# Adding an output bias on POOL ahead of time, and writing a marker one step earlier

## The chip, the cores and the metric

The kernel is one program on one core of a Trainium2 chip. Time is device microseconds of one execution, from a median of several runs; lower is better. Engines are named as in the profile: PE (TensorE), DVE (VectorE), ACT (ScalarE), POOL (GpSimd) and SP (SyncE, which here only issues DMAs). Each engine runs its own instructions strictly in the order written, and they are tied together by semaphores: an instruction adds one to a semaphore when it is done (`then_inc`), another engine waits until it has reached a value (`wait_ge`).

## What is computed

Two layers, each an attention with few keys followed by a mixture of experts (MoE), over 2048 tokens of 128 channels. Only the first attention matters here; of it, for `x` of shape (2048, 128):

```python
q = (layernorm(x) @ Wq + bq)            # 16 heads of 8 channels, each head's q scaled to length 1
attn = softmax(q @ k.T * scale + attn_bias)   # 77 keys for each of 4 batches
x = x + (attn @ v) @ Wo + bo            # bo: one row of 128 numbers, the same for all tokens
```

Behind it `layernorm(x)` goes to a router that picks 2 of 8 experts for each token.

## The kernel before

The tokens are 16 tiles of 128 (`NT`), one partition per token; `x` stays in SBUF for the whole kernel. Both attention stages are software pipelines, written as one function for each engine and step, `step0(i)` for the first stage, called for i = 0 to 23. In step i an engine works on several tiles at once: each block in the function has a line `t = i - k`, which says how many steps behind tile t stands there. The order of the blocks in the function is the order on that engine's queue, and it was laid out by hand. So each engine's step is a fixed list, and a wait in one block holds up all blocks behind it.

The blocks around the change, for tile t:

- DVE makes xnA (L918, the first LayerNorm's result) in step t + 1, from `x`. Until x's add nothing else reads `x` of that tile but this and the statistics before it.
- PE makes q, the scores S (L1378, L1381), transposes the probabilities (L1408, L1419, L1435), multiplies them with the values (L1467), and then, in step t + 7, multiplies the result with Wo into PSUM (L1428). A second product follows into the same place (L1429): a row of ones times the row `bo`, which adds the bias to all 128 tokens. Both are f32 and go as two passes each.
- DVE adds this to `x` (L902, step t + 7), takes mean and variance (L924 to L945), and makes `pays`, the normalised rows that will be sent to the experts, twice (L1018). `pays` needs rsD, the variance to the power -0.5, from POOL.
- PE transposes `pays` (L1388, step t + 8), ACT copies it to x2T (L673), PE makes the router's scores (L1459), DVE picks the two experts and counts ranks until the slot numbers of each token stand in `slots` (L1004, step t + 8).
- `pays` also has one more column, the marker, which says where the row comes from. ACT writes it from `dest` (L676, step t + 8, right behind x2T). Before that ACT waits until the scatters of tile t - 4 are done, since four buffers of `pays` go round.
- POOL scatters the rows into DRAM by the slot numbers with two indirect DMAs (L495), after waits for the marker and the slot numbers.

POOL's step in this order: rsD of tile i - 6 (L482), in steps 0 to 3 the power for four tiles of the first LayerNorm (L485), the two scatters of tile i - 7, and qr, the power -0.5 for the lengths of q, of tile i - 1 (L502). POOL's steps lie beside later ones of DVE: POOL's step i waits for what DVE makes in step i + 1 and at the start of step i + 2.

DVE's step, from L902 on: x's add, the scores minus their maximum (L908, L910), xnA, statistics and routing in turn, 1/denominator (L981, waits for PE's L1467), the attention output `on` (L998), slot numbers (L1004), `qn` (L1009, q times qr), `pays` (L1018), qsm (L876), `big` (L882), the maxima (L890, L891), q plus its bias (L896), and x's add again.

After step 23 DVE works out which expert each of 39 blocks of 128 rows belongs to, SP waits for the last scatters, and the first MoE reads the rows back. `bo_bc` holds `bo` broadcast to all 128 partitions; the kernel before uses only its first partition.

Of the kernel before, what the change touches and what calls it, by code (L numbers as in the profile page):

```python
# [34 lines left out]
ALU = mybir.AluOpType  # L35
# [9 lines left out]
def bass_xattn_moe_two_layers(nc, x_in, ctx_in, bias_in, Wq0, bq0, Wk0, Wv0, Wo0, bo0, scale_log,  # L45
                              Wr0, W1_0, W2_0, W3_0, ln_g, ln_b, cln_g, cln_b, Wq1, Wkv1, Wo1,
                              Wff1, Wff2, W1_1, b1_1, W2_1, b2_1, Wr1, br1, out):
    NBATCH, SEQ, D = x_in.shape
# [8 lines left out]
    NT = T // P  # L57
# [31 lines left out]
    with ExitStack() as ctx:  # L89
# [7 lines left out]
        x = sb("x", [P, NT, D])  # L97
# [53 lines left out]
        wo0 = sb("wo0", [P, D])  # L151
# [104 lines left out]
        class Stage:  # L256
# [11 lines left out]
            def count(self, n, v):  # L268
# [5 lines left out]
                "oh", "picks", "bef", "rank", "rsel", "slotf", "slot"]  # L274
        ONLY0 = ["q", "qb", "qsq", "qss", "qsm", "qr", "qn", "hi", "lo", "Tq", "qT", "on", "To", "oT", "Wo", "mark"]
        ONLY1 = ["c1", "comb", "ffg", "th", "gg", "ffh", "fo", "den", "norm", "scr"]
# [128 lines left out]
        def _(pool):  # L405
# [68 lines left out]
            def step0(i):  # L474
# [8 lines left out]
                if i < NT // 4:  # L483
                    pool.wait_ge(a["veA"], a.count("veA", i + 1))
                    pool.tensor_tensor(rs0[:, 4 * i:4 * i + 4], ve0[:, 4 * i:4 * i + 4], mhalf[:, 0:4], ALU.pow).then_inc(a["rsA"], 1)  # L485
                t = i - 7
                if 0 <= t < NT:
# [82 lines left out]
        def _(act):  # L570
# [54 lines left out]
            def step0(i):  # L625
# [44 lines left out]
                if 0 <= t < NT:  # L670
                    s = t % 2
                    act.wait_ge(a["Tx2"], a.count("Tx2", t + 1))
                    act.copy(x2T[s], MD[:, P:2 * P]).then_inc(a["x2T"], 1)  # L673
                    if t >= PB:
                        act.wait_ge(sent[t % PB], sent_count(0, t - PB))
                    act.copy(pay[t % PB][:, :, D:ROW].bitcast(I32), dest[:, t, :].unsqueeze(2)).then_inc(a["mark"], 1)  # L676
# [108 lines left out]
        def _(dve):  # L785
# [83 lines left out]
            def step0(i):  # L869
# [28 lines left out]
                if 0 <= t < NT:  # L898
                    s = t % 2

                    dve.wait_ge(a["Wo"], a.count("Wo", t + 1))
                    dve.tensor_tensor(x[:, t, :], x[:, t, :], MD[:, 0:D], ALU.add).then_inc(a["xa"], 1)  # L902
                t = i - 5
# [378 lines left out]
        def _(pe):  # L1282
# [81 lines left out]
            def step0(i):  # L1364
# [57 lines left out]
                if 0 <= t < NT:  # L1422
                    s = t % 2

                    if i >= NT + 6:
                        keep_busy(6, TP[1])
                    pe.wait_ge(a["oT"], a.count("oT", t + 1))
                    mm(MD[:, 0:D], oT[s], wo0[:, :], start=True, stop=False)  # L1428
                    mm(MD[:, 0:D], ones_f[0:1, :], bo_bc[0:1, :], start=False, stop=True).then_inc(a["Wo"], 1)  # L1429
                t = i - 6  # L1430
# [249 lines left out]
```

## Time and profile before

| | us |
|---|---|
| median of 3 runs | 535.7 |
| lowest, highest | 534.17, 536.98 |
| the profiled execution | 536.71 |
| its span, first to last instruction | 535.0 |

Over the whole span PE is busy 474.7 us (89%), DVE 374.8 (70%), POOL 298.4 (56%) and ACT 230.2 (43%). The first attention stage's pipeline fills from about 20 to 66 us, runs steadily to about 147 us and empties until 186 us; the first MoE's first product is at 193 us. In the profile a row of the timeline gives the start, the length and the engine of one or several merged instructions, and in brackets how long the engine was idle before it and what ended that. An idle time with "issue" is one for which the profile shows no releaser. Ends of PE's products are modelled, and instructions of DVE and ACT that follow each other without a wait overlap by up to 0.1 us in the rows.

### The profile page before, as it was taken

Reading aid. Unit: us, or ns where it says so; the run is one execution under the profiler, and the core shown is the slowest. Engines: PE = TensorE matmul, PEld = TensorE weight load, DVE = VectorE, ACT = ScalarE, POOL = GpSimd, SP = SyncE. Lnnn points to the kernel's source line nnn. Section 1 sums busy time; section 2 is a strip of 40 time slices with the busy share of each in tenths; the row PEclk is TensorE's granted clock in tenths of the full one; section 3 lists DMA queues with packets and bytes.
Section 4 is the critical chain, followed back from the end, with each engine's and each line's share of the span. In section 5 each row is a group of like instructions: output and inputs, shape, how many; then the busy total and the mean of one; then the engine's idle time right before and its main releaser. Section 6 shows DMA issues by size and latency. Waiting matters only on the chain.

```text
span 535.0 us, 11426 instructions
## 1 busy us (share of the span) xinstructions
PE 474.7 (89%) x3413; PEld 405.0 (76%) x3413; DVE 374.8 (70%) x1237; ACT 230.2 (43%) x558; POOL 298.4 (56%) x361
## 2 busy tenths in 40 slices
PE   7758998999999969999878999999999689999950
PEld 6547787888897747677656888888888589999950
DVE  3883787889885503333358999999999546767727
ACT  3444655556653525555433344343434124434410
POOL 6426438777763406677523467677675624566640
PEclk8867999999999979999998999999999979999995
DMA  8999960000000933221020001100000012222016
GB/s 216 357 345 355 370 221 22 21 16 16 22 22 21 324 101 86 84 85 43 22 70 10 21 21 35 30 31 17 17 15 22 21 49 80 69 72 64 31 39 214
DMA packets 42930, 49.16 MB, mean 92 GB/s; under 512 B 7809, under 2 KB 28636, under 8 KB 42871
## 3 DMA queue, kind: packets, MB, share of 16 engines
q1 hardware_dynamic: 36991, 39.57, 23.4%
q0 software_dynamic: 4544, 8.44, 4.8%
q10 hardware_dynamic: 1336, 0.43, 0.4%
q8 instruction: 30, 0.49, 0.4%
q14 instruction: 29, 0.24, 0.2%
HBM read 20.97 MB, written 28.35 MB: 92 GB/s over the span
## 4 chain that ended last, share of the span: by engine, by line
PE 73%; DVE 13%; POOL 4%; issue 4%; ACT 2%; DMA 2%; another core or an unknown queue 1%; SPq 0%; POOLq 0%; DVEq 0%; ACTq 0%
PE ps L1614 10%; PE ps L1467 7%; PE ps L1597 6%; PE ps L1603 6%; PE ps L1560 5%; PE ps L1538 5%; PE ps L1515 3%; PE ps L1378 3%; PE ps L1289 2%; PE ps L1552 2%; PE ps L1562 2%; PE ps L1623 2%; PE ps L1589 2%; PE ps L1381 2%; PE ps L1447 1%
## 5 line engine op out<-in xcount | busy, mean ns | idle before, releaser
L557 POOL DMA_INDIRECT ys<-ysbs,backs x78 | 76.7, 983 | 56.2 <-issue 33.5
L502 POOL TENSOR_TENSOR qr<-qsm,mhalf 128x16 f32<-128x16 f32 x16 | 47.3, 2958 | 23.7 <-DVE qsm L876 23.6
L495 POOL DMA_INDIRECT rows<-pays,slots x32 | 33.2, 1038 | 31.8 <-DVE slots L1004 21.4
L1230 DVE TENSOR_TENSOR big<-big,ps 128x256 f32<-128x256 f32 x39 | 16.4, 421 | 49.2 <-ACT big L741 46.9
L523 POOL DMA_INDIRECT rows<-pays,slots x32 | 32.7, 1023 | 19.7 <-DVE slots L1078 14.4
L746 ACT ACTIVATE big<-big 128x512 f32<-128x512 f32 x39 | 24.6, 631 | 44.3 <-issue 25.2
L514 POOL TENSOR_TENSOR pp<-pp,rden 128x1232 f32<-128x1232 f32 x16 | 36.0, 2253 | 13.4 <-DVE x L1056 10.2
L1597 PE MATMUL ps<-region_b,xsT 128*128 x78 | 41.9, 621 | 0.0
L1603 PE MATMUL ps<-xsT,wups 128*128 128x128 f32 x312 | 41.3, 276 | 0.0
L1614 PE MATMUL ps<-w2b,big 128*128 x312 | 41.1, 275 | 0.0
L1235 DVE TENSOR_TENSOR big<-ps,b1T 128x512 f32<-128x512 f32 x39 | 27.0, 692 | 18.7 <-PE ps L1603 16.4
L1467 PE MATMUL ps<-region_a,pp 128*128 128x90 f32 (+1 forms) x320 | 39.8, 280 | 0.1
L1614 PEld LDWEIGHTS ps<-w2a,big 128*128 128x128 f32 x156 | 23.1, 190 | 20.5 <-issue 18.1
L1560 PE MATMUL ps<-vals,pp 128*128 128x128 f32 x320 | 38.4, 275 | 0.0
L1614 PEld LDWEIGHTS ps<-w2b,big 128*128 128x128 f32 x312 | 37.9, 192 | 0.2 <-issue 0.2
L1603 PEld LDWEIGHTS ps<-xsT,wups 128*128 128x128 f32 x312 | 37.9, 192 | 0.0
L1467 PEld LDWEIGHTS ps<-region_a,pp 128*128 128x128 f32 x320 | 37.3, 191 | 0.7 <-issue 0.3
L1538 PE MATMUL ps<-keys,xT 128*128 128x462 f32 (+1 forms) x96 | 37.4, 527 | 0.0
L1560 PEld LDWEIGHTS ps<-vals,pp 128*128 128x128 f32 x320 | 37.0, 192 | 0.0
L1289 PE MATMUL ps<-ones_f 128*128 128x128 f32 x214 | 33.1, 316 | 1.7 <-POOL empty L409 1.7
L1289 PEld LDWEIGHTS ps<-ones_f 128*128 128x128 f32 x214 | 31.4, 230 | 2.6 <-POOL empty L409 1.7
L692 ACT COPY x2T<-ps 128x128 f32<-128x128 f32 x16 | 4.3, 267 | 65.7 <-PE ps L1491 65.7
(279 smaller groups left out, 1256.8 us busy)
## 6 DMA issues: line engine op xcount, KB each, us to landing
rows<-empty SPq DMA_DIRECT2D x68, 258.0 KB, 4.4
xs<-rows SPq DMA_DIRECT2D x78, 64.5 KB
region_b<-in_L_ffn_W_dram SPq DMA_DIRECT2D x2, 1024.0 KB, 9.7
region_a<-in_L_ffn_W_dram SPq DMA_DIRECT2D x1, 2048.0 KB
yb_all<-ys SPq DMA_DIRECT2D x16, 128.0 KB, 2.0
keys<-ys SPq DMA_DIRECT2D x8, 256.0 KB
ys<-ysbs,backs POOLq DMA_INDIRECT x78
rows<-pays,slots POOLq DMA_INDIRECT x64
```

Of the source, the lines that this page charges most:

```text
L495: pool.indirect_dma_start(rows[0][:, :], bass.IndirectOffsetOnAxis(slot[t % PB][:, k:k + 1], 0), pay[t % PB][:, k, :], None, bounds_check= ...
L502: pool.tensor_tensor(qr[s], qsm[s], mhalf[:, 0:H], ALU.pow).then_inc(a["qr"], 1)
L514: pool.tensor_tensor(p3, p3, rden[s].unsqueeze(2).to_broadcast([P, H, KEYS]), ALU.mult).then_inc(a["norm"], 1)
L523: pool.indirect_dma_start(rows[1][:, :], bass.IndirectOffsetOnAxis(slot[t % PB][:, k:k + 1], 0), pay[t % PB][:, k, :], None, bounds_check= ...
L557: pool.indirect_dma_start(ys[l][:, :], bass.IndirectOffsetOnAxis(backs[:, j % XB:j % XB + 1], 0), ysb[j % YB], None, bounds_check=2 * T - ...
L1289: mm(bank[:, 0:P], ones_f[:, :], ones_f[:, :], start=True, stop=True)
L1467: ins = mm(MC[:, h * VW:e * VW], probT[s][:, c * P:(c + 1) * P], vals0[:, t // TPB, c, h:e, :].rearrange("p h v -> p (h v)"), start=c == 0 ...
L1538: ins = mm(S[bank][:, 0:n * KEYS], xT[s], keys1[:, t // TPB, h0 * KEYS:(h0 + n) * KEYS], start=True, stop=True)
L1560: mm(MC[:, 0:D], probT[s][:, c * P:(c + 1) * P], vals1[:, t // TPB, c, :], start=c == 0, stop=False)
L1597: mm(S[s][:, :], xsT[s], w13[:, expert[t], :], start=True, stop=True).then_inc(m["up"], 1)
L1603: ins = mm(S[s][:, k * P:(k + 1) * P], wup[t % WB][:, k * P:(k + 1) * P], xsT[s], start=True, stop=True)
L1614: ins = mm((MC, MD)[s][:, 0:D], hT[s][:, k * P:(k + 1) * P], w2[:, expert[t], k, :], start=k == 0, stop=k == nk - 1)
```

## The change

Wo's bias is no longer added by a product. POOL adds `bo_bc` to `x` of tile t, a 128 x 128 addition in f32, between rsD and the scatters of its step, after a wait until xnA of this tile has been made (a new semaphore `xb` says when it is done). Wo's product is closed by itself, and DVE's add L902 waits for `xb` as well as for Wo. Besides, ACT writes the marker of tile t in step t + 7 instead of t + 8, in the same place of its list.

```diff
         def step0(i):   # POOL
...
                 if i < NT // 4:
                     pool.wait_ge(a["veA"], a.count("veA", i + 1))
                     pool.tensor_tensor(rs0[:, 4 * i:4 * i + 4], ve0[:, 4 * i:4 * i + 4], mhalf[:, 0:4], ALU.pow).then_inc(a["rsA"], 1)
+                t = i - 4
+                if 0 <= t < NT:
+                    pool.wait_ge(a["xnA"], a.count("xnA", t + 1))
+                    pool.tensor_tensor(x[:, t, :], x[:, t, :], bo_bc[:, :], ALU.add).then_inc(a["xb"], 1)
                 t = i - 7
...
         def step0(i):   # ACT
...
                     act.copy(x2T[s], MD[:, P:2 * P]).then_inc(a["x2T"], 1)
+                t = i - 7
+                if 0 <= t < NT:
                     if t >= PB:
                         act.wait_ge(sent[t % PB], sent_count(0, t - PB))
                     act.copy(pay[t % PB][:, :, D:ROW].bitcast(I32), dest[:, t, :].unsqueeze(2)).then_inc(a["mark"], 1)
...
         def step0(i):   # DVE
...
                     dve.wait_ge(a["Wo"], a.count("Wo", t + 1))
+                    dve.wait_ge(a["xb"], a.count("xb", t + 1))
                     dve.tensor_tensor(x[:, t, :], x[:, t, :], MD[:, 0:D], ALU.add).then_inc(a["xa"], 1)
...
         def step0(i):   # PE
...
                     pe.wait_ge(a["oT"], a.count("oT", t + 1))
-                    mm(MD[:, 0:D], oT[s], wo0[:, :], start=True, stop=False)
-                    mm(MD[:, 0:D], ones_f[0:1, :], bo_bc[0:1, :], start=False, stop=True).then_inc(a["Wo"], 1)
+                    mm(MD[:, 0:D], oT[s], wo0[:, :], start=True, stop=True).then_inc(a["Wo"], 1)
```

## Rows read from the trace of the kernel before

**Rows 1.** Stretches: length, then busy us of PE, PEld, DVE, ACT, POOL; clock, DMA, GB/s.

```profile
88.00:147.00 59.00, 58.78 (x462) 52.47 (x463) 52.07 (x209) 36.01 (x88) 44.54 (x32) 1.00 0.06 19
```

**Rows 2.** Chain that ended last, in order of time: start, us, what; one step.

```profile
119.85 0.41 PE ps L1429 x2
```

**Rows 3.** Timeline (start us, us, engine, line, operation, idle before), PE in one step.

```profile
119.35 0.30 PEld L1428 LDWEIGHTS ps<-wo,oT 128*128 128x128 f32 x2
...
119.78 0.48 PE L1429 MATMUL ps<-bo_bc,ones_f 1*128 1x128 f32 x2
...
120.19 0.20 PEld L1435 LDWEIGHTS ps<-ident,pp 128*128 128x128 f32 x2
...
125.05 0.14 PEld L1388 LDWEIGHTS ps<-ident,pays 128*128 128x128 f32 x1
...
126.73 0.30 PEld L1428 LDWEIGHTS ps<-wo,oT 128*128 128x128 f32 x2
```

**Rows 4.** Timeline, DVE in the same step.

```profile
120.30 0.29 DVE L902 TENSOR_TENSOR x<-x,ps 128x128 f32<-128x128 f32 x1 [0.58 <-issue]
...
121.92 0.34 DVE L918 TENSOR_SCALAR xnA<-x,mv,rs 128x128 f32<-128x128 f32 x1
...
124.22 0.15 DVE L1004 SCALAR_TENSOR_TENSOR slots<-topi,slotf 128x2 int32<-128x2 uint32 x1
...
124.49 0.41 DVE L1018 TENSOR_SCALAR pays<-x,mvD,rsD 128x256 f32<-128x256 f32 x1
```

**Rows 5.** Timeline, POOL from these slot numbers to the next rsD.

```profile
125.24 1.14 POOL L495 DMA_INDIRECT rows<-pays,slots  x1 [1.48 <-DVE slots L1004]
...
127.67 2.96 POOL L502 TENSOR_TENSOR qr<-qsm,mhalf 128x16 f32<-128x16 f32 x1
...
130.58 0.57 POOL L482 TENSOR_TENSOR rsD<-veD,mhalf 128x1 f32<-128x1 f32 x1
```

**Rows 6.** Timeline, the first slot numbers, the first scatter and the rsD behind it.

```profile
78.24 0.15 DVE L1004 SCALAR_TENSOR_TENSOR slots<-topi,slotf 128x2 int32<-128x2 uint32 x1
...
81.65 1.23 POOL L495 DMA_INDIRECT rows<-pays,slots  x1 [4.13 <-issue]
...
87.09 0.56 POOL L482 TENSOR_TENSOR rsD<-veD,mhalf 128x1 f32<-128x1 f32 x1
...
87.69 0.47 DVE L1018 TENSOR_SCALAR pays<-x,mvD,rsD 128x256 f32<-128x256 f32 x1 [0.23 <-POOL rsD L482]
```

**Rows 7.** Timeline, x's add of the 14th tile on DVE.

```profile
162.94 0.29 DVE L902 TENSOR_TENSOR x<-x,ps 128x128 f32<-128x128 f32 x1 [0.22 <-PE ps L1429]
```

**Rows 8.** POOL's groups: busy us, mean ns; then one line's min/median/max ns.

```profile
L457 POOL TENSOR_TENSOR brest<-bias_sb,pieces 128x308 f32<-128x308 f32 x1 | 0.8, 777 | 2.7 <-ACT pieces L592 2.7
...
L541 POOL TENSOR_SCALAR xnA<-x,mvA,rsA x16: 794/796/916, 273.2 to 398.0; 128x128 f32<-128x128 f32 x16
```

**Rows 9.** Timeline, DVE instructions that ran beside a POOL product, two places.

```profile
21.90 2.29 POOL L469 TENSOR_TENSOR pp<-mask,vT 128x1232 f32<-128x1232 f32 x1
21.99 2.28 DVE L918 TENSOR_SCALAR xnA<-x,mv,rs 128x128 f32<-128x128 f32 x1 [1.17 <-POOL rs L485]
...
311.29 2.25 POOL L514 TENSOR_TENSOR pp<-pp,rden 128x1232 f32<-128x1232 f32 x1 [0.75 <-DVE x L1056]
...
313.15 0.41 DVE L1078 SCALAR_TENSOR_TENSOR slots<-topi,slotf 128x2 int32<-128x2 uint32 x1
```

**Rows 10.** Timeline, tenth and eleventh slot numbers and the rsD between them.

```profile
146.37 0.15 DVE L1004 SCALAR_TENSOR_TENSOR slots<-topi,slotf 128x2 int32<-128x2 uint32 x1
...
152.74 0.55 POOL L482 TENSOR_TENSOR rsD<-veD,mhalf 128x1 f32<-128x1 f32 x1
153.20 0.15 DVE L1004 SCALAR_TENSOR_TENSOR slots<-topi,slotf 128x2 int32<-128x2 uint32 x1
```

**Rows 11.** Timeline, a marker copy on ACT and the scatter of the fifth tile.

```profile
125.66 0.20 ACT L676 COPY pays<-dest 128x2 int32<-128x2 int32 x1
...
110.48 1.15 POOL L495 DMA_INDIRECT rows<-pays,slots  x1 [1.48 <-DVE slots L1004]
```

More of the change, by code:

```diff
@@ L274, in bass_xattn_moe_two_layers @@
                 "oh", "picks", "bef", "rank", "rsel", "slotf", "slot"]
-        ONLY0 = ["q", "qb", "qsq", "qss", "qsm", "qr", "qn", "hi", "lo", "Tq", "qT", "on", "To", "oT", "Wo", "mark"]
+        ONLY0 = ["q", "qb", "qsq", "qss", "qsm", "qr", "qn", "hi", "lo", "Tq", "qT", "on", "To", "oT", "Wo", "mark", "xb"]
         ONLY1 = ["c1", "comb", "ffg", "th", "gg", "ffh", "fo", "den", "norm", "scr"]
```

## Prediction

> **What bounds the kernel now.** I read the stretches table first, to see which engine fills the stage that is changed, then the chain that ended last, then the instructions of one step in order of time, engine by engine, and last the rows that can price what is new.
>
> From 88 to 147 us, the steady part of the first attention stage, PE is busy 58.78 of 59.00 us at a granted clock of 1.00 (its upper level, 2.4 GHz), DVE 52.07, POOL 44.54, ACT 36.01 [rows 1]. The chain that ended last runs there on PE, and the bias product, two passes, has 0.41 us of it in a step [rows 2]. So PE sets the step: 7.38 us from one Wo product to the next (119.35 to 126.73). The bias product starts to load at 119.78, what follows it on PE at 120.19: it holds the queue for 0.41 us [rows 3]. DVE is idle 0.58 us in front of x's add (L902) [rows 4].
>
> Close behind PE comes POOL, and this is what the reader must see before believing the gain. The slot numbers are ready at 124.22 + 0.15 = 124.37. POOL's first scatter starts 0.87 us later (125.24), the power for q 2.43 us after that (127.67); the power rsD for the second LayerNorm starts the moment the power for q is done (130.58) and ends at 131.15, 3.48 us after that one's start. From slot numbers to the end of the next rsD: 0.87 + 2.43 + 3.48 = 6.78 us. The next slot numbers are ready at 124.37 + 7.38 = 131.75. POOL's free time is 0.6 us a step, and all of it lies between rsD and the slot numbers [rows 4, 5].
>
> **The change part by part.**
> *The bias product goes.* 0.41 us in each of 16 tiles, 6.6 us at most. In the steady part all that follows Wo on PE and DVE moves with it, since L902's idle 0.58 us covers 0.41: the step by PE becomes 6.97 us. Not all 16 count. The third tile's product (its Wo lies between the rows of 78.24 and 87.09) falls in the step where POOL's first scatter starts 3.26 us behind its slot numbers (78.39, 81.65) instead of 0.87; rsD then ends at 87.65 and the pays at 87.69 wait for it, whatever PE saves [rows 6]: 0 us. For the 14th tile DVE is idle only 0.22 us at L902, and with 0.07 us of the usual overlap of DVE instructions about 0.30 us comes out [rows 7].
>
> *POOL's add comes.* 128 x 128 in f32 with two SBUF inputs is not in the trace. Nearest rows: POOL's subtraction of 308 elements took 0.78 us, its product of 1232 elements 2.25; the line through them is 0.285 us + 1.6 ns an element, 0.49 us at 128. From above, its two-scalar operation on the same 128 x 128 took 0.80 us, at worst 0.92. From below, 128/1232 of the long product, 0.23 us. It can't be below nothing, since POOL has no such work now. I take 0.49, as the two-input rows are the same form [rows 8, 9]. The GPSIMD Engine Reference of the Trainium skill (section 3.1) gives 4497 ns for such an add of 2048 elements; with the fixed part of the two rows that makes an estimate of 0.55 us and a sum 0.5 us higher than mine, and no row here shows it.
>
> *Does it hide?* By POOL's queue alone, yes: it starts when rsD is done, and the first scatter comes only 0.87 us behind the slot numbers anyway. But POOL and DVE get in each other's way. DVE's L918, which started 0.09 us behind a POOL product, took 2.28 us instead of 0.34 and ended 0.08 us behind it. In the second attention stage the DVE instruction for the slot numbers takes 0.41 us instead of 0.15: it runs from 313.15 to 313.56, and POOL's product ends at 313.54 [rows 4, 9]. So slot numbers that come while the add runs would end 0.02 us behind it. SBUF — State Buffer of the Trainium skill (section "Who interferes with whom") says that a DVE operation with two SBUF inputs and a POOL operation that reads SBUF share a read port as an exclusive lock: the first holds it, the other fully blocks. By that rule, the two rows above agree, the change can give back most of its gain; without it the step would be 6.97.
>
> That makes a ring: slot numbers, 0.87, 2.43, 3.48, add 0.49, 0.02, next slot numbers: 7.29 us a step. The order can turn: DVE would be ready for the slot numbers at 6.72 to 6.82 us and the add starts at about 6.77. If DVE is first, the add holds up qn and the pays instead. PE takes up the pays (L1388) 0.15 us after they end, where a waiting instruction follows by about 0.05 (L902 behind the product) [rows 2 to 4], so PE has 0.1 us to give; the step would then be 6.87 and the next 7.29, in the mean 7.08. I take 7.2, between the two, and keep 7.08 and 7.29 as bounds.
>
> *Where pays wait for rsD.* In the step of the first scatter the add starts at 87.65 and the pays at 87.69: they end about 0.25 us later, once [rows 6].
>
> *The last step with a power for q.* From the slot numbers at 146.37 to those at 153.20 it is 6.83 us, and rsD ends at 153.29 only. The ring makes it 7.2: 0.37 us lost where PE would save 0.41 [rows 10]. Behind it POOL has no power for q any more and the add lies free.
>
> *The marker copy* keeps its place on ACT, between x2T and the next xT, and its 0.20 us; only its tile is the next one. It now waits for the scatters of tile t - 4 one step earlier. For the ninth tile that is where the copy of 125.66 stands now, and the scatter it needs is the one issued at 110.48, 15 us before [rows 11]. It costs 0 us; without that cover ACT's xT and with it PE's q product would wait behind it. On POOL the marker's wait is passed long before the slot numbers in either kernel. The added waits are old, too: POOL's for xnA by three steps, DVE's at L902 for the add by two; as an instruction of its own the latter may cost 0 to 0.05 us.
>
> **Sum.** Two products before the first slot numbers: -0.82. Pays behind the first scatter: +0.25. The fourth tile's product: -0.41. From the first slot numbers (78.24) to the tenth (146.37) are nine steps [rows 6, 10]; the first and the long one are in these three terms, seven remain: 7 x (7.20 - 7.385) = -1.30. The step after: +0.37. Four tiles of the tail: -0.41 - 0.30 - 0.41 - 0.41 = -1.53. In all -3.44 us. The last scatters, the schedule and all later stages start from this chain and move with it. The profiled execution (535.0 us of span, 536.7 in all) would become 531.6 and 533.3. It lies 1.0 us above the median of the three runs, 535.7, from which I forecast 532.3. At 7.29 us a step the sum is -2.7, at 7.08 it is -4.4.
>
> **Rivals.**
> *Full gain.* DVE never waits for the add. Then POOL's 6.78 us lie inside 6.97: -0.82 - 8 x 0.41 - 0.14 (the last step with a power for q can't go below 6.69, or the pays wait for rsD) - 1.53 = -5.8 us, 529.9 us. For it: 0.6 us of free time is more than the add needs, and no DVE instruction beside a short POOL operation need be hit. Against it: the free time shrinks with the step.
> *The add eats the gain.* What the add takes beyond 0.49 us counts nine times: in the eight steps of the ring and once at the pays. At 0.65 to 0.80 us the sum is -1.3 to 0.1, in the middle 535.1 us. For it: the same elements took 0.80 us [rows 8]. Against it: that form also fetches two scalars.
> *Slower.* The same ring past its turning point, which is an add of 0.79 us. At the 0.92 us of the longest such row [rows 8] nine times 0.43 us stand against 2.7: +1.2 us, 536.9 us. Against it: no two-input row of POOL lies that high for so few elements.
> *It doesn't do what it says.* The marker copy brings nothing: that is in the sum. The product is off PE in any case.
>
> **Chances.** The forecast, a ring at 7.08 to 7.29 us: 0.48. Full gain: 0.22. Eaten gain: 0.18. Slower: 0.12. A measurement of this kernel can tell about 0.5%, 2.7 us. Faster by more than that (under 533.0 us): the full gain and four fifths of the forecast, 0.60. Slower by more needs an add of 1.1 us or a cost that I don't see: 0.06. Within: 0.34. The likeliest case alone spans 531.3 to 533.0. The range takes in the full gain and most of the eaten one, and the runs of before lie 2.8 us apart: 529.3 to 535.9.
>
> **What would show it.** Right: Wo products 7.1 to 7.3 us apart between 100 and 140 us; the add at 0.49 us right behind rsD; the instruction for the slot numbers longer than its 0.15 us, or that for the pays longer than 0.41, and ending with the add; the first scatter 0.87 us behind the slot numbers; PE idle in front of L1388; the stretch from 155 us to the first MoE tile 1.5 us shorter. Steps of 6.97 speak for the full gain, of 7.4 or more for the eaten one. Wrong if the add is over 0.6 us, if DVE keeps its lengths beside it, or if a later stage's first wait gives the gain back.

## The result and the profile after

The changed kernel takes 527.12 us in the median of four runs (525.54 to 528.25), the kernel before 534.93 us in four (533.14 to 536.98): a ratio of 0.9854, 95% interval 0.9812 to 0.9896. A second comparison with six and eleven runs gave 527.10 against 535.54 us, 0.9842 (0.9814 to 0.9870). Faster was right; 7.8 us are more than twice the 3.4 us forecast, and more than the 5.8 us of the rival "full gain". 527.1 lies under the range. Both intervals lie clear of 1; the gain is under 2%.

The profiled execution took 527.4 us with a span of 525.3, against 536.71 and 535.0 before. First the busy line of the page, then the stretch 88 to 140 us of the changed kernel (columns as in [rows 1]).

```profile
PE 465.8 (89%) x3381; PEld 398.3 (76%) x3381; DVE 374.6 (71%) x1237; ACT 229.3 (44%) x558; POOL 305.8 (58%) x377
...
88.00:140.00 52.00, 52.00 (x424) 46.93 (x422) 50.14 (x197) 32.80 (x83) 44.92 (x39) 1.00 0.06 19
```

PE is still the engine that never rests, but DVE is now busy for 50.14 of 52 us. Where the step got shorter is seen in PE's weight loads, changed kernel:

```profile
105.69 0.30 PEld L1435 LDWEIGHTS ps<-wo,oT 128*128 128x128 f32 x2
...
105.91 0.26 PEld L1441 LDWEIGHTS ps<-ident,pp 128*128 128x128 f32 x2
...
106.62 0.30 PEld L1465 LDWEIGHTS ps<-wr,x2T 128*128 128x128 f32 x2
```

and in the kernel before, the load that answers to the last of these (the others are [rows 3]):

```profile
120.80 0.30 PEld L1459 LDWEIGHTS ps<-wr,x2T 128*128 128x128 f32 x2
```

From the load for Wo to the load for the router it was 120.80 - 119.35 = 1.45 us; it is 106.62 - 105.69 = 0.93. The product was worth 0.52 us, not 0.41. Two consecutive steps on DVE and POOL, changed kernel, in order of time:

```profile
103.00 0.45 POOL L489 TENSOR_TENSOR x<-x,bo_bc 128x128 f32<-128x128 f32 x1
...
103.16 0.31 DVE L1011 SCALAR_TENSOR_TENSOR slots<-topi,slotf 128x2 int32<-128x2 uint32 x1
...
104.34 1.14 POOL L499 DMA_INDIRECT rows<-pays,slots  x1 [0.89 <-DVE slots L1011]
...
106.76 2.96 POOL L506 TENSOR_TENSOR qr<-qsm,mhalf 128x16 f32<-128x16 f32 x1
...
109.68 0.56 POOL L482 TENSOR_TENSOR rsD<-veD,mhalf 128x1 f32<-128x1 f32 x1
...
110.04 0.15 DVE L1011 SCALAR_TENSOR_TENSOR slots<-topi,slotf 128x2 int32<-128x2 uint32 x1
...
110.20 0.50 POOL L489 TENSOR_TENSOR x<-x,bo_bc 128x128 f32<-128x128 f32 x1
...
110.31 0.55 DVE L1025 TENSOR_SCALAR pays<-x,mvD,rsD 128x256 f32<-128x256 f32 x1
...
111.06 1.14 POOL L499 DMA_INDIRECT rows<-pays,slots  x1 [0.36 <-issue]
```

The add costs 0.45 to 0.50 us. In the first step it is ahead of the slot numbers, which take 0.31 us instead of 0.15 [rows 4] and end at 103.47, 0.02 us behind the add. In the second, the slot numbers slip in before the add starts, and the pays are held instead: 0.55 us instead of 0.41, ending at 110.86 where the add ends at 110.70. Both orders of the prediction are there, side by side. At the first scatter:

```profile
75.52 0.15 DVE L1011 SCALAR_TENSOR_TENSOR slots<-topi,slotf 128x2 int32<-128x2 uint32 x1
...
76.73 1.23 POOL L499 DMA_INDIRECT rows<-pays,slots  x1 [1.40 <-issue]
```

It starts 1.06 us behind its slot numbers (75.67), where it was 3.26 us in before [rows 6]. That was in no term of the sum.

**The account.** The same marks in both profiles (DVE's second xnA at the pipeline's start, the slot numbers of each tile, the last copy of a gathered tile in the second MoE), in us:

| stretch | before | after | difference | forecast |
|---|---|---|---|---|
| start to second xnA | 36.25 | 34.70 | -1.55 | 0 |
| to first slot numbers | 41.99 | 40.82 | -1.17 | -0.82 |
| first to third slot numbers | 16.45 | 13.81 | -2.64 | -0.16 |
| third to tenth (seven intervals) | 51.68 | 48.44 | -3.24 | -1.30 |
| tenth to eleventh | 6.83 | 6.50 | -0.33 | +0.37 |
| eleventh to sixteenth | 29.63 | 28.54 | -1.09 | -1.53 |
| all behind the last slot numbers, to the last gathered tile | 327.54 | 327.78 | +0.24 | 0 |

The sum is -9.8 us in the two profiled executions. The first line turns out below to be chance, and without it -8.2 us stand against the -7.8 and -8.4 us of the medians. The second line varies as well: over all profiles it is 40.9 and 41.5 to 42.1 us with the product and 40.7 to 41.0 without it (the 40.9 is the second profile of before).

### The profile page after: what moved, and what is told of

Read it like the earlier page. It is cut to its first block, busy times and chain, and to the rows that moved or that the text cites. A ratio compares the mean times of both kernels' runs of the same rounds, so it can differ in the third digit from the quotient of the medians.

```text
span 525.3 us, 11394 instructions
## 1 busy us (share of the span) xinstructions
PE 465.8 (89%) x3381; PEld 398.3 (76%) x3381; DVE 374.6 (71%) x1237; ACT 229.3 (44%) x558; POOL 305.8 (58%) x377
## 3 DMA queue, kind: packets, MB, share of 16 engines
q0 software_dynamic: 4544, 8.44, 4.9%
## 4 chain that ended last, share of the span: by engine, by line
PE 75%; DVE 13%; POOL 4%; issue 2%; DMA 2%; ACT 2%; SPq 0%; POOLq 0%; DVEq 0%; ACTq 0%
PE ps L1620 10%; PE ps L1473 7%; PE ps L1603 7%; PE ps L1609 6%; PE ps L1566 6%; PE ps L1544 5%; PE ps L1521 3%; PE ps L1385 3%; PE ps L1296 3%; PE ps L1558 2%; PE ps L1568 2%; PE ps L1595 2%; PE ps L1629 2%; PE ps L1388 2%; PE ps L1453 1%
```

## The experiments

Each kernel's profile gives three numbers that are compared throughout: the plain step (between slot numbers in the steady part), the third tile's interval (which holds the first scatter), and the stretch from the first slot numbers to the last, 15 intervals.

| kernel | plain step | second to third slot numbers | first to last slot numbers | first scatter behind slot numbers |
|---|---|---|---|---|
| before | 7.38 | 9.06 | 104.59 | 3.26 |
| before, second profile | 7.38 | 13.05 | 109.64 | 3.54 |
| changed | 6.92 | 6.93 | 97.29 | 1.06 |
| changed, second profile | 6.92 | 6.92 | 97.14 | 1.06 |
| product_out | 6.88 | 9.60 | 99.44 | 3.86 |
| add_only | 7.38 | 7.39 | 102.92 | 1.06 |
| mark_only | 7.38 | 9.13 | 104.65 | 3.32 |
| pad8 | 7.38 | 7.39 | 102.93 | 1.06 |
| pad1 | 7.38 | 9.08 | 104.62 | 3.28 |
| pad2 | 7.38 | 7.39 | 102.92 | 1.06 |
| pad4 | 7.38 | 7.38 | 102.89 | 1.05 |
| out_pad8 | 6.88 | 6.89 | 96.64 | 1.06 |
| k128_form | 7.10 | 10.64 | 102.35 | 3.41 |
| add_behind_scatters | 6.93 | 7.20 | 97.87 | 1.06 |
| add_twice | 7.21 | 7.47 | 100.28 | 1.07 |
| bias_early | 6.87 | 6.87 | 96.62 | 1.05 |

### The change taken apart

**product_out** leaves the bias product out of the kernel before, and the bias with it.

```diff
-mm(MD[:, 0:D], oT[s], wo0[:, :], start=True, stop=False)
-mm(MD[:, 0:D], ones_f[0:1, :], bo_bc[0:1, :], start=False, stop=True).then_inc(a["Wo"], 1)
+mm(MD[:, 0:D], oT[s], wo0[:, :], start=True, stop=True).then_inc(a["Wo"], 1)
```

> The kernel before without Wo's bias product and without any other place for the bias: Wo's bias is left out of the output, nothing is added on POOL, the marker copy stays. Theory 1 (the product costs PE 0.51 us a step, more than its own 0.41, since Wo's load of weights is followed faster without it): steps of 6.85 to 6.9 us between 100 and 140 us and no stretched slot or pays instruction, about 6.5 to 7.5 us less in all if the first scatter keeps its late start. Theory 2 (most of what went beyond the forecast is the first scatter's start, which the added POOL instructions or the marker moved): the first scatter stays 3.3 us behind its slot numbers here. Rival (the product's price is 0.41 us, and the 0.1 us came from elsewhere): steps of 6.97 us.

Measured: 0.9873 of before (0.9808 to 0.9938). The step is 6.88 us, 0.50 under before, so the product's price is 0.50 to 0.51 us with nothing else changed. The long interval stays, and is longer still (9.60), since PE comes to it sooner and waits 2.40 us:

```profile
79.54 1.23 POOL L495 DMA_INDIRECT rows<-pays,slots  x1 [4.64 <-issue]
...
86.11 0.33 PE L1388 MATMUL ps<-ident,pays 128*128 128x128 f32 x1 [2.40 <-DVE pays L1018]
```

**add_only** keeps the product and lets POOL add a row of zeros to x in the place of the new add.

```diff
+pool.wait_ge(a["xnA"], a.count("xnA", t + 1))
+pool.tensor_tensor(x[:, t, :], x[:, t, :], empty[:, 0, 0:D], ALU.add).then_inc(a["xb"], 1)
```

> The kernel before with its bias product and its marker order, and with POOL's 128 x 128 add in the place of the change, adding a row of zeros, so that the output stays whole. Theory 1: POOL's ring of about 7.25 us lies inside PE's 7.38, so the steps stay at 7.38 us and the DVE instructions for slots and pays keep 0.15 and 0.41 us, except where rsD is late: 0 to 0.5 us slower by the add alone. Theory 2 with the added POOL instructions as the cause: the first scatter starts about 1.1 us instead of 3.3 us behind its slot numbers and the whole is 1.5 to 2 us faster. If the marker is the cause, the first scatter stays 3.3 us behind and nothing is faster.

Measured: 0.9990 of before (0.9964 to 1.0015). The long third interval is gone, with the product still there: the stretch is 104.59 - 102.92 = 1.67 us shorter. In its 16 steps only one instruction for slot numbers (0.28 us) and one for pays (0.55) was held. The ratio's interval includes 1, so it is the profile that shows the gain, not the whole time.

**mark_only** moves the marker copy alone.

```diff
 act.copy(x2T[s], MD[:, P:2 * P]).then_inc(a["x2T"], 1)
+t = i - 7
+if 0 <= t < NT:
```

> The kernel before with nothing but the marker copy one step ahead. Theory 1 and my forecast: no change in time, within 0.3 us, steps of 7.38 us. Rival (the marker brings the first scatter forward): first scatter about 1.1 us behind its slot numbers, 2 us faster in all.

Measured: 0.9982 (0.9952 to 1.0012); its numbers are those of before within 0.1 us. The marker brings nothing that these runs can tell.

**pad8, pad1, pad2, pad4** are the kernel before with so many one-element writes on POOL ahead of its first step, into a tile that nobody reads.

```diff
+if l == 0:
+    for _ in range(8):
+        pool.memset(spare2[:, _:_ + 1], 0.0)
 for i in range(NT + LAG[l]):
```

> The kernel before with eight one-element memsets on POOL in front of its first step, 20 us before the first scatter, where POOL waits anyway. They do nothing but move the later POOL instructions by eight places in its instruction stream. Theory 2 in its sharper form (the 2 us at the first scatter are a fetch of POOL's instructions that falls between the slot numbers and the scatter): the first scatter starts about 1.1 us behind its slot numbers and the whole is about 2 us faster, with steps of 7.38 us. Rival (the delay belongs to the first scatter itself, or to the marker): it stays 3.3 us behind, no change.

> The kernel before with one one-element write on POOL ahead of the first step. Eight of them took the first scatter's delay from 3.3 to 1.06 us. Theory (a fixed place in the instruction stream where the next block of POOL's instructions is fetched, which falls just ahead of the first scatter in before): one more instruction may or may not be enough; the first scatter is either over 3 us or 1.06 us behind, nothing between, and an instruction packet lies in the 3 us ahead of it in the first case and not in the second. Rival (it is the time that POOL has been busy, not the place): 3.3 us again for one, two and four writes alike.

> The same with two writes. Theory: as with one; if one is enough, two are. If the place sits at the scatter's own instructions, the delay goes at one particular number and stays away up to eight. Rival: 3.3 us.

> The same with four writes, as many as the changed kernel has adds on POOL ahead of its first scatter. Theory: 1.06 us behind the slot numbers, no long third interval (7.39 in place of 9.06 to 10.2), the instruction packet some us later. Rival: 3.3 us, so that the changed kernel's gain here comes from something other than the number of instructions.

Measured: pad8 0.9974 (0.9940 to 1.0007), an interval that includes 1; pad1, pad2 and pad4 have one run each (534.11, 532.15 and 533.84 us), too little for a ratio. What they show, they show in their profiles. With one write the delay is there, with two, four and eight it is gone, and nothing lies between 1.06 and 3.28. The other kernels fit this count: k128_form has one write more than before ahead on POOL and is late, bias_early_no_writes has two large adds, add_behind_scatters three adds and the changed kernel four, and all three are on time. The scatter and its slot numbers of pad1, then of pad2 (timelines):

```profile
77.72 0.15 DVE L1008 SCALAR_TENSOR_TENSOR slots<-topi,slotf 128x2 int32<-128x2 uint32 x1
...
81.15 1.23 POOL L496 DMA_INDIRECT rows<-pays,slots  x1 [4.16 <-issue]
```

```profile
77.44 0.15 DVE L1008 SCALAR_TENSOR_TENSOR slots<-topi,slotf 128x2 int32<-128x2 uint32 x1
...
78.65 1.23 POOL L496 DMA_INDIRECT rows<-pays,slots  x1 [1.94 <-issue]
```

The traffic of queue 14, "instruction", goes with it. In slices of 0.2 us, before has one packet of it from 79.6 us, 1.2 us behind the slot numbers (78.39) and 2.05 us ahead of the scatter (81.65):

```profile
q14 instruction: 1, 0.01, 11.3%
```

In all six profiles with the delay (both of before, mark_only, product_out, pad1, k128_form) a packet lies 1.2 to 1.4 us behind the slot numbers and the scatter starts 2.0 to 2.5 us behind the packet; another follows 2.6 to 3.3 us after the first. Around the slot numbers pad2 has none until 82.0 us, the changed kernel none until 79.1, 2.4 us after its scatter. Against a simple link speak the versions with the early bias, further down: two of them have a packet 0.1 us ahead of and 0.3 us behind the slot numbers' end, 1.1 and 0.75 us ahead of a scatter that is on time. That the late packet brings the next instructions of POOL, which waits for them, is my reading and not shown; that the delay hangs on how many instructions stand ahead on POOL, and not on what the added work is, is what the writes show.

**out_pad8** puts both causes together: no product, no bias, no add, eight writes; its diff is that of product_out and that of pad8.

> The kernel before without the bias product and without any add of the bias (the bias is not in the output), and with eight one-element writes on POOL ahead of the first step. It puts two causes together that ran apart: the product (0.51 us a step) and the late first scatter (2.1 us). Theory (the two are separate and add up): steps of 6.80 to 6.89, first scatter 1.06 us behind its slot numbers, no wait of PE behind it; the ratio is that of the version without the product (0.9873) less 0.4%, about 0.983, that is the changed kernel's 0.984 to 0.985 within 0.2%, so that POOL's adds cost 0 to 1 us in all. Rival: the changed kernel has yet another gain, and this one stays 2 us or more above it.

Measured: 525.66 us, 0.9816 (0.9794 to 0.9838), a stretch of 96.64 us. Against pad8 the product's absence alone is worth 102.93 - 96.64 = 6.29 us there. The changed kernel's 97.29 and 97.14 are 0.5 to 0.65 us more: that is all that sixteen adds on POOL cost in this stretch. By the medians (0.9842 to 0.9854 against 0.9816) they cost 1.4 to 2.0 us, more than the 0 to 1 expected, with intervals that overlap. There is no third gain. By the stretch the change comes apart as 104.59 - 102.93 = 1.66 us for the first scatter on time, 6.29 for the product, and 0.65 back for the adds, 7.30 in all.

### Why the product is dearer than its own time

**k128_form** keeps the product but gives it 128 rows: 1/128 times the bias in every partition.

```diff
-mm(MD[:, 0:D], ones_f[0:1, :], bo_bc[0:1, :], start=False, stop=True).then_inc(a["Wo"], 1)
+mm(MD[:, 0:D], ones_p[:, :], bo_bc[:, :], start=False, stop=True).then_inc(a["Wo"], 1)
```

> The kernel before, with the bias product in another form: a 128 x 128 block of 1/128 times the bias in all 128 partitions, in place of one row of ones times one row of bias. The same number of products, no add on POOL. With the bias product the steps are 7.38 us, without it 6.88. Theory 1: half of the 0.51 us is the one-row form itself: the weight loads before and behind it (0.43 and 0.41 us) do not follow at the pace of a 128-row pair; then with 128 rows both products take about 0.45 to 0.5 us in place of 0.84, the step falls to about 7.05 to 7.15, and the kernel ends about 4 us ahead of the one before. Rival: two float32 products take what they take in any form; the step stays at 7.38 and the time is that of before within 0.3%.

Measured: 0.9916 (0.9893 to 0.9939), 4.5 us faster than before with the same number of products. Its loads:

```profile
119.72 0.30 PEld L1430 LDWEIGHTS ps<-wo,oT 128*128 128x128 f32 x2
119.94 0.30 PEld L1431 LDWEIGHTS ps<-bo_bc,ones_p 128*128 128x128 f32 x2
120.17 0.25 PEld L1437 LDWEIGHTS ps<-ident,pp 128*128 128x128 f32 x2
```

The loads for Wo, the bias and the next transposes start 0.22 and 0.23 us apart; in before it is 0.43 and 0.41 [rows 3]. The step falls to 7.10: of the product's 0.51 us, 0.28 come from its one-row form, which slows the neighbouring pair too, and 0.23 from the two passes.

### Where the add stands, and how much room it has

**add_behind_scatters** moves POOL's add from ahead of the scatters to behind them.

```diff
-pool.tensor_tensor(x[:, t, :], x[:, t, :], bo_bc[:, :], ALU.add).then_inc(a["xb"], 1)
 t = i - 7
...
+t = i - 4
+pool.tensor_tensor(x[:, t, :], x[:, t, :], bo_bc[:, :], ALU.add).then_inc(a["xb"], 1)
 t = i - 1
```

> The changed kernel, with the add of the bias moved on POOL from ahead of the scatters to behind them, ahead of the power for q. Theory 1 (the add is free only because POOL waits for the slot numbers there): behind the scatters there is no wait, so the add's 0.49 us joins POOL's own round from slot numbers to the second power: 6.9 us grows to about 7.2 to 7.4, DVE waits for the second power ahead of pays, slot numbers take 0.15 us each since nothing runs beside them on POOL, steps of 7.2 to 7.4 us in place of 6.92, and the kernel is 4 to 6 us slower than the changed one. Rival: POOL has slack of over 0.5 us in its round wherever the add stands; steps of 6.9 and the time of the changed kernel within 0.3%.

Measured: 530.94 us, 0.9839 (0.9794 to 0.9883), the ratio of the changed kernel. Theory 1 falls: steps of 6.94, not 7.2 to 7.4. Its trace shows why POOL's longer round hardly shows. DVE's pays now wait for rsD in each step:

```profile
118.94 0.15 DVE L1011 SCALAR_TENSOR_TENSOR slots<-topi,slotf 128x2 int32<-128x2 uint32 x1
119.46 0.41 DVE L1025 TENSOR_SCALAR pays<-x,mvD,rsD 128x256 f32<-128x256 f32 x1 [0.16 <-POOL rsD L482]
...
119.96 1.23 POOL L495 DMA_INDIRECT rows<-pays,slots  x1 [0.54 <-issue]
...
122.48 0.48 POOL L500 TENSOR_TENSOR x<-x,bo_bc 128x128 f32<-128x128 f32 x1
...
125.81 0.55 POOL L482 TENSOR_TENSOR rsD<-veD,mhalf 128x1 f32<-128x1 f32 x1
...
126.39 0.41 DVE L1025 TENSOR_SCALAR pays<-x,mvD,rsD 128x256 f32<-128x256 f32 x1 [0.17 <-POOL rsD L482]
```

From the slot numbers (118.94) it is 1.02 us to the scatter, from there 6.43 to the pays behind the next rsD (126.39), and from the pays to the slot numbers after that about 6.42 (119.46 to 125.88 one step earlier): 13.87 us, two steps of 6.94. A way round that ends at the same instruction always comes to whole steps, so the sum doesn't say what bounds. It does say that the way takes two steps. I had counted POOL's work as if it returned to the same instruction after one. DVE still waits 0.16 us for Wo ahead of x's add, where it is 0.17 in bias_early, and the step is only 0.07 us longer than there.

**add_twice** puts a second add of the same size behind the first.

```diff
+pool.tensor_tensor(twice[:, :], bo_bc[:, :], empty[:, 0, 0:D], ALU.add).then_inc(twos, 1)
```

> The changed kernel with a second add of the same size behind the first on POOL, into a tile that nobody reads: about 0.5 us more on POOL in the same place. It asks how much of POOL's wait for the slot numbers is left. Theory 1 (my sum put the round at 7.1 to 7.3 us with one add, the changed kernel showed 6.9, so little is left): the second add runs into the slot numbers' time in every step, the round is 7.2 to 7.5 us, steps of 7.2 to 7.5, 4 to 8 us slower than the changed kernel. Rival: the wait has room for a second add, steps stay at 6.9 to 7.0, and the time is within 0.3% of the changed kernel's.

Measured: 530.83 us, 0.9852 (0.9826 to 0.9878). The steps are 7.21 us, at the low end of theory 1, and the stretch is 3.0 us longer than the changed kernel's. The whole time doesn't show these 3 us: the ratio is that of the changed kernel from other sets of runs, and beside bias_early, of the same set, it is 2.0 us more where the stretches differ by 3.7. Where the rest went is open. One step on POOL with the slot numbers:

```profile
112.75 0.54 DVE L1016 SCALAR_TENSOR_TENSOR slots<-topi,slotf 128x2 int32<-128x2 uint32 x1
...
114.16 1.14 POOL L504 DMA_INDIRECT rows<-pays,slots  x1 [0.36 <-issue]
...
116.58 2.96 POOL L511 TENSOR_TENSOR qr<-qsm,mhalf 128x16 f32<-128x16 f32 x1
...
119.50 0.57 POOL L484 TENSOR_TENSOR rsD<-veD,mhalf 128x1 f32<-128x1 f32 x1
...
119.96 0.54 DVE L1016 SCALAR_TENSOR_TENSOR slots<-topi,slotf 128x2 int32<-128x2 uint32 x1
...
120.02 0.46 POOL L491 TENSOR_TENSOR x<-x,bo_bc 128x128 f32<-128x128 f32 x1
120.43 0.59 POOL L494 TENSOR_TENSOR twice<-bo_bc,empty 128x128 f32<-128x128 f32 x1
...
121.37 1.15 POOL L504 DMA_INDIRECT rows<-pays,slots  x1 [0.36 <-issue]
```

This is the ring of the prediction, closed in every step: slot numbers (113.29), 0.87 to the scatter (114.16), 2.42 to qr (116.58), 3.44 to the add (120.02), 0.46 for the first add, and the slot numbers end 0.02 to 0.03 us behind it (120.50): 7.21 us. The second add stands in none of these terms. What it does is hold the pays as well, 0.54 us instead of 0.41 in each steady step; PE then waits 0.37 us for them, and the next slot numbers come late enough to meet the add again. That this wait is what makes them late is read from the trace, not tested. In the changed kernel's steady part a held step is followed by one or more in which the slot numbers come first.

POOL's 0.36 us of idle time, put down to "issue", is a wait for the slot numbers: the scatter starts 0.87 us behind their end here as in the steady steps of all kernels. Where POOL itself is the late one, the gap is only 0.18 us:

```profile
84.70 0.51 POOL L494 TENSOR_TENSOR twice<-bo_bc,empty 128x128 f32<-128x128 f32 x1
...
85.40 1.05 POOL L504 DMA_INDIRECT rows<-pays,slots  x1 [0.18 <-issue]
```

From scatter to the end of the second add it is 6.85 us (114.16 to 121.01), with 0.18 that makes 7.03 us of POOL's own work. With one add it is 6.36 (104.34 to 110.70) and 6.54. So one add leaves POOL's own work about 0.3 us to spare against 6.87, and even two don't make it the bound at 7.21.

### The add out of the steps

**bias_early** makes x + bo for all tiles with two large adds on POOL, before the steps that have slot numbers, into space that is free then; DVE's residual add reads that. Six one-element writes keep up the number of POOL's instructions; bias_early_no_writes is the same without them.

```diff
+pool.wait_ge(ld["x"], 16)
+for h in range(2):
+    pool.tensor_tensor(xpb[:, 8 * h:8 * h + 8, :], x[:, 8 * h:8 * h + 8, :],
+                       bo_bc[:, :].unsqueeze(1).to_broadcast([P, 8, D]), ALU.add).then_inc(A[0]["xb"], 1)
...
-dve.tensor_tensor(x[:, t, :], x[:, t, :], MD[:, 0:D], ALU.add).then_inc(a["xa"], 1)
+dve.tensor_tensor(x[:, t, :], xpb[:, t, :], MD[:, 0:D], ALU.add).then_inc(a["xa"], 1)
```

> The changed kernel, but the bias is added to all of x by two large adds on POOL before the first step with slot numbers, into space that is free by then; VectorE's residual add reads that copy. No add is left in the steps on POOL; six one-element writes keep the number of POOL's instructions ahead of the first scatter near that of the changed kernel. Theory 1 (the block beside the slot numbers costs 0.05 us a step): steps of 6.87 to 6.88 each, slot numbers 0.15 us throughout, 0.5 to 1 us faster than the changed kernel. Rival A: the two large adds (about 2048 elements' worth of columns, some 4 us) run beside VectorE's first steps and hold it: 1 to 4 us slower than the changed kernel, all of it before the fourth step. Rival B: the first scatter goes 3 us behind its slot numbers again, +2.1 us.

> The version with two large adds ahead of the steps, once more, against the changed kernel of the same call. Steps of 6.87 us against a mean of 6.9: over the 15 intervals about 0.5 us faster than the changed kernel. The two large adds held POOL from 29.6 to 34.2 us and the powers for the first LayerNorm with it; if that counts, it gives back 0.5 us and the two are the same within 0.3%.

> The changed kernel once more, beside the version with the bias added early on the same chip. Steps of 6.7 to 7.2 us with a mean of 6.9 and the first scatter 1.06 us behind its slot numbers. The second variance of the first LayerNorm on VectorE (0.17 us in the one profile of the changed kernel, 1.76 in the one of before) shows whether the prologue differs from one execution to the next in the same kernel: theory, it may be anything from 0.17 to 2 us here; rival, it is 0.17 again and belongs to the change. Time 1.2 to 1.8% under the kernel before.

> The same without the six one-element writes on POOL. Nothing is computed otherwise; only the number of POOL instructions ahead of the first scatter falls by six. Theory (the long start of the first scatter depends on where in POOL's instruction stream it stands, and an extra packet on the instruction queue comes just ahead of it): the first scatter is 3.2 to 3.9 us behind its slot numbers again, the third interval 9.0 to 9.7 us in place of 6.87, and the kernel 2 to 2.7 us slower than with the writes. Rival (what removed the delay was something else, such as POOL being busy in the steps before): 1.06 us as with the writes, and no difference.

Measured: bias_early 528.85 us, 0.9831 (0.9794 to 0.9868), beside add_twice; then, side by side with the changed kernel, 525.35 against 527.10 us (0.9820 with 0.9790 to 0.9849, against 0.9842 with 0.9814 to 0.9870), and without the writes 526.16 (0.9832, 0.9802 to 0.9862). In the profiles the steps are 6.87 us flat, no DVE instruction for slot numbers or pays is held, and the stretch is 96.62 us in each of the three profiles, 0.5 to 0.7 us under the changed kernel, as theory 1 had it. DVE waits for Wo in each step again:

```profile
114.29 0.29 DVE L914 TENSOR_TENSOR x<-wups,ps 128x128 f32<-128x128 f32 x1 [0.17 <-PE ps L1440]
```

The two large adds can cost something ahead of the steps: in the first profile of bias_early DVE's two products `pp` beside them took 4.33 us instead of 2.78, in the other two profiles the adds were done before (rival A, in one execution of three). The intervals of the two ratios overlap, so that this version is faster is shown for the stage, not for the whole. The expectation for the version without the writes failed: its first scatter is on time as well (1.05 us). Two more adds on POOL ahead are then enough, as two writes are in pad2; my guess that six fewer instructions would bring the delay back was wrong because it takes the count of before, or one more, to have it.

### Once more the kernel before

> The kernel before once more, for a second profile. Steps of 7.38 us, the first scatter 3.2 to 3.4 us behind its slot numbers (81.65 against 78.39 in the first profile), third interval 9.06. The second variance on VectorE: 1.76 us in the first profile; theory, between 0.17 and 2 here, by the execution; rival, 1.76 again.

Measured: 537.28 us, one run. The third interval is not 9.06 us but 13.05, and the next 8.44, together 6.7 us more than two plain steps. The stretches and PE's wait of that profile:

```profile
86.68 0.33 PE L1389 MATMUL ps<-ident,pays 128*128 128x128 f32 x1 [1.80 <-DVE pays L1019]
```

```profile
84.00:86.00 2.00, 0.88 (x6) 0.51 (x5) 0.29 (x1) 0.03 (x1) 2.00 (x2) 1.00 0.00 0
86.00:88.00 2.00, 1.32 (x10) 1.13 (x11) 1.84 (x5) 1.33 (x6) 1.52 (x3) 1.00 0.11 29
88.00:90.00 2.00, 2.00 (x10) 1.55 (x9) 0.64 (x3) 0.87 (x2) 1.99 (x2) 0.53 0.15 45
...
96.00:98.00 2.00, 2.00 (x10) 1.38 (x9) 1.72 (x9) 0.41 (x1) 0.19 (x1) 0.50 0.00 0
98.00:100.00 2.00, 2.00 (x15) 1.66 (x14) 1.01 (x2) 0.86 (x5) 1.70 (x2) 0.91 0.10 33
```

PE stood 1.80 us for the pays that the late scatter held up, and from 88 to 98 us the granted clock was 0.50 to 0.53, the lower level, 1.2 GHz. In k128_form the same wait (1.90 us) was followed by 0.68 and 0.50 from 88 to 92 us; its third interval is 10.64. In before (1.46 us), pad1 (1.48), mark_only (1.51) and product_out (2.40) the clock stayed at 1.00. So the late scatter costs 1.7 us in the kernel before when the clock holds, and up to 6.7 when it doesn't. With the scatter on time PE waits for the third pays by 0.1 us at most, in add_behind_scatters and add_twice 0.4 and 0.6, and in all twelve such profiles the clock stayed at 1.00 from 84 to 94 us.

The second variance of the first LayerNorm, ahead of the pipeline, in this profile and in the changed kernel's second:

```profile
25.40 0.17 DVE L965 TENSOR_SCALAR ve<-mv 128x4 f32<-128x4 f32 x1
```

```profile
26.29 0.92 DVE L972 TENSOR_SCALAR ve<-mv 128x4 f32<-128x4 f32 x1
```

It had been 1.76 us in before's first profile and 0.17 in the changed kernel's. In before it began at 25.50 us beside a POOL product that ran from 24.99 to 27.24, and that product starts when a PSUM tile arrives for it in that execution; over all profiles it took 0.17 to 2.20 us with no relation to the version. The 1.55 us of the account's first line are such luck: in the second profiles the same stretch is 35.50 us in before and 36.20 in the changed kernel, the other way round.

## Why the prediction was wrong, and where it was right

Three terms of the sum failed, and all three on the same side; one was the ring, the case that the forecast was named for. Line by line against the account, leaving out its first line, the forecast missed 4.8 us: about 2.4 at the first scatter, 1.9 by the ring (in eight intervals), 1.1 by the product's price (in the eleven tiles where PE's step counted), and the tail and the later stages take 0.7 back. The way it was to go, faster, was right.

**The product's price (0.41 us a step): the first step that failed.** I took the distance from the bias product's load to the next one's and let the chain of waits confirm it with its 0.41 [rows 2, 3]. Both leave out what the one-row product does to its neighbours: Wo's load was followed after 0.43 us, where 128-row pairs follow after 0.22. It could have been read in before: there the same chain gives the two transposes behind the bias product 0.37 us, while the 128-row transposes of L1394 and L1399 take 0.11 each:

```profile
118.09 0.11 PE ps L1394
118.19 0.11 PE ps L1399
...
119.85 0.41 PE ps L1429 x2
120.26 0.37 PE ps L1435 x2
```

0.41 + 0.37 - 0.22 is 0.56, near the 0.51 that product_out showed; in its chain the same two transposes take 0.22 us. The 0.10 us count where PE's step counted: in two tiles ahead of the first slot numbers, the fourth, the seven of the steady part and the one behind them, 1.1 us in all.

**The first scatter's delay was taken as a constant: the second step that failed.** I saw the 3.26 us [rows 6] and wrote "whatever PE saves", but didn't ask what made it late when every one from the third tile on came 0.87 us behind its slot numbers. An idle time of 4.13 us on it, where its like in the steady part has 1.48, was the sign. (That it is put down to "issue" is none by itself: the scatters that are on time in the changed kernel show "issue" too, with 0.36 and 1.40 us.) It hung on how many instructions stand ahead on POOL, which the change raised. Worth 1.67 us with the product there; without the product it is 99.44 - 96.64 = 2.80 us, since PE's saving can't pass the delay. The account's third line shows -2.64 against my -0.16.

**The ring (7.20 us a step): its parts were right, that it bounds every step was not; the third step that failed.** Scatter 0.87 us behind the slot numbers, 2.42 to qr, 3.48 to the end of rsD, the slot numbers held until 0.02 us behind the add: all of it measured as forecast, and the alternation too (slot numbers 6.72 and then 7.22 us apart, ending at 103.47, 110.19 and 117.41). But I priced the pair as 6.87 and 7.29. A held instruction shifts the slot numbers by 0.3 us against PE's beat, and the next ones come back to the beat, so a hold is not added to the step. PE's steps (by x's add) were 6.88 to 6.96 us, 6.92 in the mean: the block costs 0.05 us a step and not the 0.23 by which 7.20 lies over 6.97. Of the 0.28 us a step by which the account's fourth line was missed, this is 0.18 and the product 0.10. The ring is no fiction: in add_twice, where the slot numbers are held in every step, it closes at 7.21 us, beside the 7.29 of the prediction. The hold takes what room DVE has: the idle time ahead of six of x's adds between 97 and 138 us was 3.5 us in before, is 1.0 with the bias added early, and 0.4 in the changed kernel (groups by line, DVE, of before and then of after; the last figure is the idle time).

```profile
L902 DVE TENSOR_TENSOR x<-x,ps 128x128 f32<-128x128 f32 x6 | 1.7, 288 | 3.5 <-issue 3.5
```

```profile
L909 DVE TENSOR_TENSOR x<-x,ps 128x128 f32<-128x128 f32 x6 | 1.7, 287 | 0.4 <-PE ps L1435 0.3
```

The "full gain" rival was right that the add costs little (0.5 to 0.65 us in the stretch), but built on the same 0.41 and the same fixed delay.

**The add (0.49 us): right.** 0.44 to 0.50 us in nearly all steps. The estimate of 0.55 us that I worked out by the GPSIMD Engine Reference of the Trainium skill (section 3.1) was further off. The eaten gain and the slower case needed 0.65 us and more, and are out.

**The lock: right in kind.** SBUF — State Buffer of the Trainium skill ("Who interferes with whom") has the later of the two operations wait until the first is done, and the slot numbers that end 0.02 us behind the add agree. For the pays it agrees less well: they ran 0.14 us long where the add covered 0.39 of their 0.55 us (110.31 to 110.70).

**The tenth interval and the tail.** +0.37 forecast, -0.33 measured: the same ring that didn't bound. The tail gave -1.09 where I had -1.53: its five intervals fell by 0.03, 0.33, 0.33, 0.41 and 0.00 us. I had given the 14th tile 0.30 for DVE's 0.22 us at x's add; the 12th and 13th show the same 0.22 in before. In the first of the five an instruction for slot numbers is held (0.35 us), and the last is 3.49 us in both kernels.

**The marker at 0 us: right** (mark_only). **Later stages give nothing back: right.** From the last slot numbers to the last gathered tile it is 324.6 to 329.0 us over all profiles, 326.9 in the mean of the eight that keep the one-row product and 327.0 in the mean of nine without it. It also shows how far two single profiles may differ for nothing.

**What had been named as a sign against.** Steps of 6.97 were to speak for the full gain and 7.1 to 7.3 for the forecast; 6.92 is below both, which could only come from a product that costs more than 0.41. It was the steps, not the total, that told this first.

## What to carry to other kernels

Price the removal of an instruction by the distance between its neighbours against the same pair elsewhere, not by its own row. A wait that is long at one instance only of a repeated instruction is an open question, not a constant, and an edit anywhere ahead on that engine can remove it or bring it. A short hold on an engine with slack shifts its work against the beat of the engine that bounds; count a ring by the number of steps after which it closes, and ask what makes it close in the next step too, before taking its length for the step.

## What the runs showed of the hardware

- A bias product of one row in f32 costs 0.51 us between 128-row products, the same product with 128 rows 0.22 to 0.23: the loads ahead of and behind the one-row pair come 0.43 and 0.41 us apart instead of 0.22.
- POOL's first scatter came 3.3 to 3.9 us or 1.06 us behind its slot numbers, by whether zero and one or two and more instructions had been put ahead of it; in the late case a packet on an instruction queue lay about 2 us ahead of it.
- A wait of PE of 1.5 to 2.4 us in a busy stage was followed by the lower clock in two of six profiles (waits of 1.80 and 1.90 us), for about 10 and 3 us, and not in four, the longest wait among them.
- Of two instructions that can't run side by side, one of DVE and one of POOL, which one is held changed from step to step in the changed kernel, and either order lengthened the step by under 0.1 us. With a second add behind the first both the slot numbers and the pays were held in every step, and it was 0.34 us longer.
- An indirect scatter of POOL starts 0.87 us behind the end of the slot numbers it waits for, in the steady steps of every kernel here, also where the profile puts the idle time down to "issue"; where POOL is the late one it follows its predecessor by 0.18 us.
